# Value and residual projections: two slots share one load of x, six projection matmuls in place of eight

## What is computed

```python
B, F = (2048, 40)          # EMB = 64, HEADS = 4, ATT = 32, OUT = 128
q = (einsum('bfe,oe->bfo', x, Wq) + bq).reshape(B, F, H, D)
k = (einsum('bfe,oe->bfo', x, Wk) + bk).reshape(B, F, H, D)
v = (einsum('bfe,oe->bfo', x, Wv) + bv).reshape(B, F, H, D)
att = softmax(einsum('bfhd,bghd->bhfg', q, k) / sqrt(64), axis=-1)
out = einsum('bhfg,bghd->bfhd', att, v).reshape(B, F, H * D)
res = einsum('bfe,oe->bfo', x, Wr) + br
return relu(out + res)
```

## Time and profile before

| | |
|---|---|
| median of three executions | 938.09 us (936.63 to 940.19) |
| the profiled execution | 944.5 us, its span 942.4 us |
| busy: PE | 916.0 us, 97% |
| busy: POOL | 876.5 us, 93% |
| busy: ACT, DVE | 769.2 us (82%), 726.7 us (77%) |
| granted TensorE clock, mean | 0.995 |
| DMA | 101.20 MB, 107 GB/s |

### The profile page before, as it was taken

How to read it: one execution, slowest core, us unless ns; L and a number is a source line. 1 busy time by engine, 2 the same in 40 slices (tenths; PEclk the granted TensorE clock), 3 DMA queues, 4 the chain that set the end, 5 groups by cost and what they waited for, 6 DMA issues and landing times.

```text
span 942.4 us, 68912 instructions
## 1 busy us (share of the span) xinstructions
PE 916.0 (97%) x30720; PEld 680.3 (72%) x30720; DVE 726.7 (77%) x2066; ACT 769.2 (82%) x1541; POOL 876.5 (93%) x1028
## 2 busy tenths in 40 slices
PE   6999999999999999999999999999999999999996
PEld 4777777777777777777777777777777777777774
DVE  6777777778777877777777777777778777777775
ACT  4888888888887888878888788887888888888885
POOL 3999999999998999989999999999999999999997
PEclk9999999999999999999999999999999999999997
DMA  4333333333333333333333333333333333333321
GB/s 117 100 108 109 108 115 110 109 110 115 108 107 105 109 109 108 110 104 107 116 108 110 108 109 114 112 109 102 115 109 109 114 105 116 109 109 106 108 77 65
DMA packets 67433, 101.20 MB, mean 107 GB/s; under 512 B 13632, under 2 KB 46656, under 8 KB 67136
## 3 DMA queue, kind: packets, MB, share of 16 engines
q1 hardware_dynamic: 66704, 96.65, 33.7%
q10 hardware_dynamic: 432, 0.15, 0.1%
HBM read 54.81 MB, written 41.94 MB: 103 GB/s over the span
## 4 chain that ended last, share of the span: by engine, by line
PE 97%; issue 2%; ACT 0%; DMA 0%; DVE 0%; POOL 0%; POOLq 0%; ACTq 0%
PE vr_bank L429 24%; PE o_bank L461 22%; PE s_buf L402 19%; PE o_bank L382 14%; PE s_buf L438 10%; PE vr_bank L419 6%; PE vr_bank L431 1%; DMA biases<-bias_in 0%; PE o_bank L386 0%; POOL y_sum L187 0%; ACT rv L254 0%; ACT y_rows L234 0%; POOLq L35 0%; ACT q_flat L227 0%; PE vr_bank L424 0%
## 5 line engine op out<-in xcount | busy, mean ns | idle before, releaser
L179 POOL TENSOR_TENSOR m_diag<-m_split,ident 128x640 bf16<-128x640 bf16 x256 | 322.2, 1258 | 49.7 <-DVE m_split L332 35.2
L187 POOL TENSOR_TENSOR y_sum<-rv,y_att 128x512 f32<-128x512 f32 x256 | 302.9, 1183 | 1.9 <-DVE y_att L343 1.9
L195 POOL TENSOR_SCALAR q_bd<-q_flat,consts 128x320 f32<-128x320 f32 x512 | 265.8, 532 | 10.8 <-DVE kT L316 10.8
L431 PE MATMUL vr_bank<-w_cols,xT 64*128 64x128 f32 x2048 | 270.9, 273 | 0.0
L429 PE MATMUL vr_bank<-w_cols,xT 64*128 64x128 f32 x2048 | 270.7, 273 | 0.0
L254 ACT ACTIVATE rv<-vr_bank 128x1024 f32<-128x1024 f32 x256 | 260.1, 1016 | 0.0
L321 DVE TRANSPOSE_TENSOR_REDUCE s_buf<-s_buf 128x20 f32<-128x640 f32 x256 | 221.5, 865 | 46.2 <-PE s_buf L402 46.2
L429 PEld LDWEIGHTS vr_bank<-w_cols,xT 64*128 64x128 f32 x2048 | 251.2, 190 | 0.0
L431 PEld LDWEIGHTS vr_bank<-w_cols,xT 64*128 64x128 f32 x2048 | 250.4, 189 | 0.0
L461 PE MATMUL o_bank<-rv,pT 64*40 64x33 f32 x16384 | 225.0, 202 | 10.3 <-issue 8.3
L402 PEld LDWEIGHTS s_buf<-q_bd,kT 64*40 64x40 f32 x8192 | 150.9, 112 | 116.0 <-issue 115.0
(11 more groups left out here) (33 smaller groups left out, 624.1 us busy)
## 6 DMA issues: line engine op xcount, KB each, us to landing
xT<-xT_in SPq DMA_DIRECT2D x512, 104.0 KB, 2.5
y<-y_rows SPq DMA_DIRECT2D x512, 80.0 KB
w_cols<-w_in SPq DMA_DIRECT2D x1, 128.0 KB, 2.2
vr_bias<-vr_bias_in ACTq DMA_DIRECT2D x1, 128.0 KB, 3.4
consts<-consts_in ACTq DMA_DIRECT2D x1, 20.0 KB, 2.0
biases<-bias_in ACTq DMA_DIRECT2D x1, 1.0 KB, 3.7
```

Source lines behind the costliest of these rows:

```text
L179: pool.tensor_tensor(m_diag[:], m_split[:, place % 2].unsqueeze(2).to_broadcast([P, BLOCKS, QUAD]), ident[:].unsqueeze(1).to_broadcast([P, ...
L187: pool.tensor_tensor(y_sum[:, n % 3].rearrange("r (a d) -> r a d", d=DIM), rv[:, place % 4, 1, :, 0:DIM], y_att[:, place % 2].rearrange("r ...
L195: pool.tensor_scalar(q_bd[:, place % 4, :, s], q_flat[:, place % 2].rearrange("d (b f) -> d b f", f=FIELDS), consts[:, C_HEAD + s:C_HEAD + ...
L431: mm = nc.tensor.matmul(vr_bank[:, 1, OUT * pair:OUT * (pair + 1)], xT[HALF:P, place % 8, cols], w_cols[HALF:P, 1], start=False, stop=True ...
```

## The change

Values and residual of a slot were computed from two loads of x, one in either row half, four slots each. Now each row half computes one slot with both Wv and Wr from one load (256 moving columns) and two slots with one of the two (128 moving columns). The lower half gives the values of slots 0, 1 and 2 and the residual of slot 2; the upper half gives the residuals of slots 0, 1 and 3 and the values of slot 3. w_cols has a third block for this, so that Wv, Wr or Wr, Wv stand side by side. Where member and output half were crossed in one slot of each two, they are now crossed in slots 0 and 1 and straight in slots 2 and 3. In `attend` the bank is chosen by crossed or straight and no longer by the member. The sizes of ACT's, DVE's and POOL's operations in a step stay as they are; four one-time copies at the start write 32 columns for 16.

```diff
-ORDER = [MEMBERS * slot + member for member in range(MEMBERS) for jj in range(2)
-         for slot in (2 * jj + member, 2 * jj + 1 - member)]
+CROSSED = 2
+ORDER = [MEMBERS * slot + (member ^ (slot < CROSSED)) for slot in range(SLOTS) for member in range(MEMBERS)]
+VALUES, RESIDUAL = (0, 1, 2, 7), 3
...
-        w_cols = sb("w_cols", [P, 2, OUT])
+        w_cols = sb("w_cols", [P, 3, OUT])
...
-                pool.tensor_tensor(y_sum[...], rv[:, place % 4, 1, :, 0:DIM],
+                pool.tensor_tensor(y_sum[...], rv[:, place % 4, RESIDUAL * HEADS:(RESIDUAL + SLOTS) * HEADS, 0:DIM],
...
-                nc.scalar.copy(rv[:, i, 0, :, DIM:VW],
-                               consts[...].to_broadcast([P, SLOTS * HEADS, 1])).then_inc(prepared, 1)
+                nc.scalar.copy(rv[:, i, :, DIM:VW],
+                               consts[...].to_broadcast([P, 2 * SLOTS * HEADS, 1])).then_inc(prepared, 1)
...
+                def blocks(half, first, step):
+                    return vr_bank[:, half].rearrange("r (a c) -> r a c", c=OUT)[:, first::step]
+
+                def project(half, pair, first, step, count):
+                    rows = slice(HALF * half, HALF * (half + 1))
+                    return nc.tensor.matmul(blocks(half, first, step)[:, 0:count],
+                                            xT[rows, place % 8, PAIR * pair:PAIR * pair + P],
+                                            w_cols[rows, 1:1 + count],
+                                            start=False, stop=True, skip_group_check=True)
...
-                nc.tensor.matmul(vr_bank[:, 0, 0:2 * OUT], bias_pick[0:HALF], bias_rows[0:HALF].rearrange("r s c -> r (s c)"),
+                nc.tensor.matmul(blocks(0, 0, 2), bias_pick[0:HALF], bias_rows[0:HALF],
                                  start=True, stop=False, skip_group_check=True)
...
-                nc.tensor.matmul(vr_bank[:, 1].rearrange("r (m j c) -> r m j c", m=MEMBERS, j=2)[:, :, 1],
-                                 bias_pick[HALF:P], bias_rows[HALF:P],
+                nc.tensor.matmul(blocks(1, 0, 2), bias_pick[HALF:P], bias_rows[HALF:P],
                                  start=True, stop=False, skip_group_check=True)
-                for pair in range(SLOTS):
-                    cols = slice(PAIR * pair, PAIR * pair + P)
-                    nc.tensor.matmul(vr_bank[:, 0, OUT * pair:OUT * (pair + 1)], xT[0:HALF, place % 8, cols],
-                                     w_cols[0:HALF, 1], start=False, stop=True, skip_group_check=True)
-                    mm = nc.tensor.matmul(vr_bank[:, 1, OUT * pair:OUT * (pair + 1)], xT[HALF:P, place % 8, cols],
-                                          w_cols[HALF:P, 1], start=False, stop=True, skip_group_check=True)
+                for pair in range(CROSSED):
+                    project(0, pair, pair, 1, 1)
+                    project(1, pair, 1 + pair, 1, 1)
+                project(0, 2, 2, 1, 2)
+                mm = project(1, 3, 0, 3, 2)
                 mm.then_inc(vr_made, 1)
...
-                for jj in range(2):
+                for idx in range(2):
                     for h in range(HEADS):
-                        for low in range(2):
+                        for c, slot in ((0, CROSSED + idx), (1, idx)):
                             for member in range(MEMBERS):
-                                slot = 2 * jj + low
-                                g = member ^ low
+                                g = member ^ c
                                 at = (2 * slot + h % 2) * FIELDS
-                                mm = nc.tensor.matmul(o_part[HALF * g:HALF * g + FIELDS, member, jj * HEADS + h],
+                                mm = nc.tensor.matmul(o_part[HALF * g:HALF * g + FIELDS, c, idx * HEADS + h],
                                                       pT[HALF * member:HALF * (member + 1), place % 2, h // 2, at:at + FIELDS],
-                                                      rv[HALF * member:HALF * (member + 1), place % 4, 0, slot * HEADS + h],
+                                                      rv[HALF * member:HALF * (member + 1), place % 4, VALUES[slot] * HEADS + h],
                                                       start=True, stop=True, skip_group_check=True)
```

More of the change, by code:

```diff
@@ L65, in attention_kernel @@
         pT = sb("pT", [P, 2, 2, TOK])
-        rv = sb("rv", [P, 4, 2, SLOTS * HEADS, VW])
+        rv = sb("rv", [P, 4, 2 * SLOTS * HEADS, VW])
         m_swap = sb("m_swap", [P, 2, BLOCKS])
@@ L186, in add_residual @@
                     pool.wait_ge(y_ready, n - 2)
-                pool.tensor_tensor(y_sum[:, n % 3].rearrange("r (a d) -> r a d", d=DIM), rv[:, place % 4, 1, :, 0:DIM],
+                pool.tensor_tensor(y_sum[:, n % 3].rearrange("r (a d) -> r a d", d=DIM), rv[:, place % 4, RESIDUAL * HEADS:(RESIDUAL + SLOTS) * HEADS, 0:DIM],
                                    y_att[:, place % 2].rearrange("r (a d) -> r a d", d=DIM),
@@ L219, in _ @@
             for i in range(4):
-                nc.scalar.copy(rv[:, i, 0, :, DIM:VW],
-                               consts[:, C_REAL:C_REAL + 1].unsqueeze(2).to_broadcast([P, SLOTS * HEADS, 1])).then_inc(prepared, 1)
+                nc.scalar.copy(rv[:, i, :, DIM:VW],
+                               consts[:, C_REAL:C_REAL + 1].unsqueeze(2).to_broadcast([P, 2 * SLOTS * HEADS, 1])).then_inc(prepared, 1)
             def queries(n, place):
@@ L253, in values_and_residual @@
                     act.wait_ge(sum_ready, n - 3)
-                nc.scalar.activation(rv[:, place % 4].rearrange("k t a v -> k (t a) v")[:, :, 0:DIM],
+                nc.scalar.activation(rv[:, place % 4, :, 0:DIM],
                                      vr_bank[:].rearrange("k t (a d) -> k (t a) d", d=DIM),
@@ L514 @@
         "xT_in": xT.reshape(steps, P, PAD),
-        "w_in": np.ascontiguousarray(np.stack([np.concatenate([Wq.T, Wk.T]), np.concatenate([Wv.T, Wr.T])], 1)),
+        "w_in": np.ascontiguousarray(np.stack([np.concatenate([Wq.T, Wk.T]), np.concatenate([Wv.T, Wr.T]),
+                                               np.concatenate([Wr.T, Wv.T])], 1)),
         "bias_in": np.ascontiguousarray(np.stack([bq, bk], 1)),
@@ L525 @@
     r = run_bass_kernel_spmd(nc, [arrays], core_ids=[0])
-    rows = r.results[0]["y"].reshape(steps, 2, FIELDS, MEMBERS, 2, OUT)
-    y = np.empty((steps, 2, 2, MEMBERS, FIELDS, OUT), np.float32)
-    for member in range(MEMBERS):
-        for low in range(2):
-            y[:, :, low, member] = rows[:, low ^ member, :, member].transpose(0, 2, 1, 3)
+    rows = r.results[0]["y"].reshape(steps, 2, FIELDS, SLOTS, OUT)
+    y = np.empty((steps, SLOTS, MEMBERS, FIELDS, OUT), np.float32)
+    for slot in range(SLOTS):
+        for member in range(MEMBERS):
+            crossed = slot < CROSSED
+            y[:, slot, member] = rows[:, member ^ crossed, :, slot + 2 if crossed else slot - 2]
     return y.reshape(batch, FIELDS, OUT)
```

## The result

The changed kernel takes 928.89 us (median of four executions, 927.11 to 929.51); the kernel before took 938.58 us on the same chip (median of four). The ratio is 0.9895, with a 95% interval from 0.9871 to 0.9919: 9.7 us or 1.05% less.

The account below looks back on a forecast made before the run. PE was taken to bound the kernel, with POOL close below. Projections 2.8 us plus fetches 1.6 less 0.3 at the start gave 4.1 us less, 938.1 to 934.0 us; range 929 to 939.5 us.

Parts of the forecast that it names:

- What bounds the kernel: PE, busy in 97% of the span, sets the step; POOL is the floor under it at 3.42 us a step.
- the place of the stalls: PE's "issue" stalls at borders of 256-instruction blocks would move by 12 matmuls a step, before by 8.
- The projection term: Projections: a wide record takes 0.217 us for two narrow ones' 0.2226; 0.011 us a step, 2.8 us less.
- The fetch term: PE's instruction fetches: more time between block borders in dense stages makes late blocks 0.035 us less late; 1.6 us less.
- The start: Program start: w_cols grows from 128 to 192 KB and may delay the first loads; 0.3 us more, 1.1 at most.
- Attention: `attend`: row halves writing one bank might take turns, so the kernel gets slower, up to about 1,126 us; chance 0.08.
- The quarter of the stage: Projections: if loads of x set the pace, two of eight intervals go, POOL then bounds, 918 us; chance 0.04.
- The fetch rival for more gain: Instruction fetches: borders visit other places, stalls sum to a fifth less, 5 us, time down to 930 us; chance 0.10.

Follow-up runs that it names:

- bias kernels: Kernel before with the lower half's bias matmul writing 320, 384 or 512 columns for 256, the added ones zeros: 940.50, 945.24 and 953.90 us beside 941.35.
- split8: Changed kernel's layout, order and banks, but each wide projection as two of 128 columns with a load each: 941.07 us beside 941.35 before, ratio 1.0012.
- after14: Changed kernel with the lower half's bias matmul 34 columns wider (zeros), undisturbed step 3.500 us as before: 933.02 us beside 943.22, ratio 0.9881.
- after14_b: Changed kernel with the lower half's bias matmul 34 columns wider, run again on another chip: 926.88 us beside 929.48 before, ratio 0.9959.
- bias348: Kernel before with 348 bias columns, 240 instructions a step, same time between block borders in `attend` as `after14_b`: 935.50 us beside 929.48, ratio 1.0061.
- store1: Kernel before storing one output row of each 40, moving 60.28 MB in place of 101.20: 927.86 us beside 937.64, ratio 0.9896.

## Why the prediction came out as it did

*What bounds the kernel, and the place of the stalls:* right. PE sets the step, and the borders move by 12 matmuls in place of 8.

*The projection term:* right in mechanism, a little small. I had 0.011 us a step and 2.8 us; the step is 0.0147 us shorter, 3.8 us, and the later start takes 0.25 of that. The wide record costs the 0.217 us that I had. Against two narrow ones of 0.1117 that is 0.0063 us each, 0.0126 a step, and the other 0.0025 come from the record behind them (0.2692 for 0.2717 us), of which I had nothing. Columns set the pace: (0.2717 - 0.1117) / 192 is 0.00083 us a column at a granted clock of 1.00, 0.1067 us for 128, so a narrow record carries 0.005 us on top and a wide one 0.004. The Trainium skill, "TensorE: Matmul & The Clock Gate", section "LDWEIGHTS (loading the stationary operand)", has a load of 128 columns take 107 ns, and the estimate worked out from it, 0.015 us a step, agrees with the trace's 0.0147. Whether it is the loads that set the narrow intervals no run here shows.

*The fetch term:* the step that failed. "26 us in all are then about 90 stalls, and 90 x 0.035 = 3.2 us is the most that this returns" holds the number of stalls fixed and shortens each. Counted over the steps from the fifth on, a step being stalled when it is over 0.015 us longer than an undisturbed one, the traces have 100 stalls of 0.252 us in the mean before and 57 of 0.218 us after. Each is indeed 0.034 us shorter, but that is the small part. The number nearly halves. The traced execution of the kernel before lay 6 us above its median, so in the medians the fall is smaller, from 20.4 to 14.4 us: the term is 6.0 us, where I took 1.6 and gave 3.2 as the bound. Why the number falls, the table above shows: two fifths of the packets landed over 2.4 us after the border before, now a fifth do, and each stall that goes saves its whole length, not the little by which its packet was late, and seems to make the next less likely. The growth of the interval was over-sized as well: records inside `attend` start 0.0096 us apart and not the stage's mean of 0.0117, so it grew there by 4 x 0.0096 - 0.0147 = 0.024 us, not 0.035. How much of the fall is the longer interval at work and how much one stall bringing fewer others isn't separated. The bound was none: it took the stalls shown, 0.16 to 0.50 us, as if each were the lateness of its block, and did not ask how many blocks stand close to being late. The same slip made the expectations of the bias kernels too hopeful in the other direction: there I carried the halving over to an interval grown by the same amount, and got 4.0 us for 12.

*The start:* 0.3 us taken. L433 now starts at 8.79 us where L419 started at 8.54, 0.25 us later.

*The rivals.* Attention keeps its 0.75 us: the lower and the upper row half may write one bank at different partitions, side by side, at no cost. The sentence of the Trainium skill, "TensorEngine Tiling (Array Packing)", section "Gotcha 1: PSUM Pressure", that different row tiles cannot access one bank at one time, is thus too wide for this case. The narrower one of the Trainium skill, "PSUM — Partial Sum Buffer", section "PSUM bank collisions raise a hardware error", which has two row tiles collide in the same bank and quadrant of partitions, fits; no run here tries one quadrant from both halves. The quarter of the stage did not go. The fetch rival for more gain, given 0.10, is nearest to what happened, though for another reason than I named there: not other places, but a longer interval.

*What is shown and what is open.* Shown: the merge and not the layout makes the gain (`split8`); the stalls are packets of instructions that land late (the table of landings); the gain survives when the step is as long as before (`after14`, 10.2 us on one chip; `after14_b`, 2.6 us on another); extra work on PE comes back in part (bias kernels); at one interval the count makes no difference that stands out of 1.6 us of scatter (`after14_b`, `bias348`); the kernel's own transfers make about half of the stalls (`store1`). Open: what the 1.06 us or more before a packet starts and the 1.4 us after its landing consist of, and why the chips differ. The kernel of `after14` and `after14_b` is one; its undisturbed step was 3.500 us on either chip, and its mean step 3.560 us where the kernel before took 943.22 us and 3.535 where it took 929.48. The median time of its fetched packets was 1.11 and 1.01 us. That fits, but I changed nothing to test it.

## What to carry to other kernels

Where an unrolled program's instructions are fetched while it runs, find where its idle time of "issue" falls and count instructions a step: a stage of dense small instructions can outrun the fetch, and then each instruction less can be worth more than its own time. Estimate what such a threshold costs by how many events stand near it and by what crossing it costs at once, and not by the mean size of those seen. A change that touches it should be judged with the work held equal (as in `after14`), since adding work gave back 40 to 58% of its cost here and can hide what is tested.

## What I had not expected of the hardware

- The kernel before took from 929.5 to 943.2 us on four chips, 1.5%, with the same clock (0.995 to 0.997). The traces of one kernel on two of them (`after14`, `after14_b`) put the whole difference into the stalls.
- An instruction of two waits on PE's queue, for a semaphore long reached, costs 0.063 us when 24 stand in a step, and PE is idle for 0.60 of these 1.518 us even with the projections' long matmuls ahead; 8 in a step gave 1014 us beside 941 for the kernel before.
- A block of 256 instructions that lands just late costs PE 0.11 to 0.15 us at once in the median, and PE goes on 1.43 us (scatter 0.09) after its packet has landed.
- Two fifths of the DMA traffic less (`store1`) gave as much time, 9.8 us, as the change under study.
